# Summing two sets of squares on TensorE as two accumulated terms, in place of an addition on GpSimd

## The reference

```python
q = q / jnp.linalg.norm(q, axis=-1, keepdims=True)        # heads of 64 channels
...
o = jnp.moveaxis(O, 0, 1).reshape(Bx, Lx, NH, HD)
o = o * jax.lax.rsqrt(jnp.mean(o * o, axis=-1, keepdims=True) + EPS) * g
out = o.reshape(Bx, Lx, NH * HD) @ Wo
```

## Time and profile before

| | |
|---|---|
| three runs, median (lowest to highest) | 1305.85 us (1302.28 to 1309.93) |
| the profiled execution | 1308.97 us |
| its span, first to last instruction | 1307.2 us |
| TensorE busy, matmuls | 1155.9 us (88%), 9320 records |
| TensorE busy, weight loads | 979.8 us (75%) |
| VectorE busy | 698.1 us (53%) |
| ScalarE busy | 622.1 us (48%) |
| GpSimd busy | 364.5 us (28%), 294 instructions |
| mean granted TensorE clock | 0.926 |

### The profile page before, as it was taken

The page is one execution under the profiler, slowest core; times in us unless marked ns, Lnnn a source line. Parts: engine busy times, 40 slices in busy tenths (PEclk is TensorE's granted clock), DMA queues, the critical chain, the costliest instruction groups (busy, mean ns, idle before and its releaser), DMA issues.

```text
span 1307.2 us, 25625 instructions
## 1 busy us (share of the span) xinstructions
PE 1155.9 (88%) x9320; PEld 979.8 (75%) x9321; DVE 698.1 (53%) x1195; ACT 622.1 (48%) x1117; POOL 364.5 (28%) x294
## 2 busy tenths in 40 slices
PE   2696889999989899878899899999999999995886
PEld 1465668778777778767788788999999999993665
DVE  2668766765666666666788523333333333333444
ACT  2665546656465646456444634444444444441221
POOL 0315333334252425222012111111111112116542
PEclk9787878999899989989999999999999999997888
DMA  3112020102020102254222411111111111134443
GB/s 123 49 33 65 7 67 17 58 9 73 9 73 10 57 3 95 73 177 141 64 73 84 135 34 34 50 50 49 48 48 48 48 48 48 48 93 134 138 129 102
DMA packets 59529, 86.37 MB, mean 66 GB/s; under 512 B 7233, under 2 KB 49089, under 8 KB 59329
## 3 DMA queue, kind: packets, MB, share of 16 engines
q1 hardware_dynamic: 52160, 65.42, 15.7%
q0 software_dynamic: 7296, 19.93, 5.6%
HBM read 60.16 MB, written 25.17 MB: 65 GB/s over the span
## 4 chain that ended last, share of the span: by engine, by line
PE 68%; DVE 17%; ACT 6%; issue 5%; POOL 2%; DMA 0%; SPq 0%; DVEq 0%; ACTq 0%; POOLq 0%
PE ps L1365 25%; PE ps L1345 23%; DVE W L1523 4%; PE ps L1202 4%; PE ps L1192 3%; PE ps L1356 3%; PE ps L1264 2%; PE ps L1271 2%; PE ps L1423 2%; DVE late_room L1705 1%; DVE W L1615 1%; PE ps L1325 1%; POOL W L804 1%; PE ps L1176 1%; PE ps L1307 1%
## 5 line engine op out<-in xcount | busy, mean ns | idle before, releaser
L1365 PE MATMUL ps<-W,late_room 128*128 (+1 forms) x3264 | 388.5, 278 | 19.6 <-issue 19.0
L1345 PE MATMUL ps<-late_room,W 128*128 128x256 f16 x3072 | 369.6, 280 | 36.2 <-DVE late_room L1705 20.9
L1365 PEld LDWEIGHTS ps<-W,late_room 128*128 128x128 f16 x3264 | 324.9, 100 | 71.3 <-issue 28.3
L1345 PEld LDWEIGHTS ps<-late_room,W 128*128 (+1 forms) x3072 | 305.9, 100 | 87.3 <-DVE late_room L1705 26.0
L1068 ACT ACTIVATE ps<-ps 128x512 f32<-128x512 f32 x272 | 158.7, 583 | 407.4 <-PE ps L1345 358.5
L1705 DVE SCALAR_TENSOR_TENSOR late_room<-ps,late_room 128x512 f16<-128x512 f32 x272 | 181.5, 688 | 249.2 <-ACT late_room L1073 230.7
L1073 ACT ACTIVATE late_room<-ps 128x512 f16<-128x512 f32 x272 | 155.8, 596 | 2.5
L1523 DVE SCALAR_TENSOR_TENSOR W<-W 128x512 f32<-128x512 f32 x144 | 122.1, 849 | 8.7 <-ACT W L941 5.3
L1202 PE MATMUL ps<-W 128*128 128x512 f16 x384 | 101.5, 409 | 1.5 <-DVE W L1699 1.5
L922 ACT COPY W<-ps 128x512 f32<-128x512 f32 x112 | 61.0, 589 | 46.8 <-PE ps L1264 34.6
L904 POOL DMA_INDIRECT W<-ys_d,pos_i x64 | 62.1, 970 | 56.4 <-DVE W L1902 18.3
(11 more groups left out here) (178 smaller groups left out, 1375.4 us busy)
## 6 DMA issues: line engine op xcount, KB each, us to landing
wstage<-in_w_ffn SPq DMA_DIRECT2D x40, 512.0 KB, 3.7
ys_d<-late_room SPq DMA_DIRECT2D x36, 256.0 KB
late_room<-in_x SPq DMA_DIRECT2D x8, 512.0 KB, 4.8
W<-in_x SPq DMA_DIRECT2D x8, 512.0 KB, 4.2
x2n_d<-W SPq DMA_DIRECT2D x8, 512.0 KB, 3.2
base_d<-W SPq DMA_DIRECT2D x8, 512.0 KB, 4.1
late_room<-base_d SPq DMA_DIRECT2D x16, 256.0 KB
acc_d<-late_room SPq DMA_DIRECT2D x12, 256.0 KB
```

What stands on the lines that cost most here:

```text
L1345: last = pe.matmul(up_bank(n, c)[:, f * XT:(f + 1) * XT], weight(slot, d, hw, cols), x_halves[:, hx, d], start=(q == 0), stop=(q == len(pa ...
L1365: last = pe.matmul(down_bank(b)[:, c * D:(c + 1) * D], hs[b][:, hh, f, c * P:(c + 1) * P], weight(slot, DB + f // 4, hw, cols), start=(q = ...
```

## The change

GpSimd's addition goes, with its semaphore `o_sq`. `head_sums` takes any number of terms and accumulates them in PSUM, so that TensorE runs two matmuls, one on `qsqT` and one on `osqT`, where it ran one on their sum. TensorE itself now waits for ScalarE's two semaphores. The call for K ("ssq") still has one term.

```diff
-                if slot == 3:
-
-                    pool.wait_ge(q_sq, DB * (n + 1))
-                    pool.wait_ge(o_own_sq, DB * (n + 1))
-                    pool.tensor_tensor(osqT, osqT, qsqT, ALU.add).then_inc(o_sq, 1)
...
-            def head_sums(dst, src):
+            def head_sums(dst, *terms):
 
                 for k in range(GT):
                     for d in range(DB):
                         at = k * NH + d * (P // HD)
-                        last = pe.matmul(dst[:, at:at + P // HD], src[:, d, k * P:(k + 1) * P], headsel,
-                                         start=True, stop=True)
+                        for q, src in enumerate(terms):
+                            last = pe.matmul(dst[:, at:at + P // HD], src[:, d, k * P:(k + 1) * P], headsel,
+                                             start=(q == 0), stop=(q == len(terms) - 1))
                 return last
...
                 if slot == 5:
 
-                    pe.wait_ge(o_sq, n + 1)
-                    head_sums(fill(tl, n, "oss"), osqT).then_inc(tl.sem_full, 1)
+                    pe.wait_ge(q_sq, DB * (n + 1))
+                    pe.wait_ge(o_own_sq, DB * (n + 1))
+                    head_sums(fill(tl, n, "oss"), qsqT, osqT).then_inc(tl.sem_full, 1)
```

More of the change, by code:

```diff
@@ L502, in build @@
         o_ready = sem("o_ready")
-        o_sq = sem("o_sq")
         o_rms = sem("o_rms")
```

## The result

In twenty runs each the changed kernel takes 1303.4 us (1299.27 to 1305.62) and the kernel before 1306.2 (1302.28 to 1311.62): ratio 0.9971, 95% interval 0.9958 to 0.9984. The forecast was 1311, 5 us more than before; it is 2.8 us less. Two later measurements on two other chips, on which both kernels are 3% faster, gave 0.9949 (0.9931 to 0.9967) and 0.9945 (0.9926 to 0.9964). So the change is a small gain of 0.3 to 0.6%, and the sign of the forecast was wrong.

The account below looks back on a forecast made before the run. TensorE's chain from K's head sums to the turned K, made late by VectorE's block, was taken as the bound. 18.8 - 8.3 - 2.5 - 3.0 = +5.0 us on the median 1305.85 gave 1311 us, range 1301 to 1319.

Parts of the forecast that it names:

- What bounds the kernel: TensorE's work from K's head sums to the turned K is the chain; GpSimd's addition costs mostly by blocking VectorE.
- The added matmuls, 18.8 us: In each group's oss, 8 more matmuls (16 records) on TensorE's chain cost 18.8 us in all.
- The block, 8.3 us: VectorE's convolution step no longer held by the addition in groups 0 to 5, so ScalarE's silu comes earlier: 8.3 us gained.
- The wait in group 7, 2.5 us: TensorE no longer waits for GpSimd's addition before oss in group 7: 2.5 us gained.
- The clock, -3.0 us: TensorE's granted clock: fewer falls after ssq, some new ones after oss, longer low stretches in groups 0 and 1; net -3.0 us.
- two and a half of the four falls gone (-6.9), two new ones (+3.4): Clock falls at ssq in groups 2 to 5 partly vanish, -6.9 us; two new falls after oss cost +3.4 us.
- The half microsecond for longer low stretches: In groups 0 and 1 the low-clock stretches last longer, costing half a microsecond.
- clock holds: Rival: no clock fall left in groups 2 to 5, oss of groups 0 and 1 at full clock; 1299.5 us, chance 0.19.
- with groups 0 and 1 as they are, -3, 1303: Milder case: no fall left in groups 2 to 5, groups 0 and 1 unchanged; -3 us, 1303 us, within the rival's 0.19.
- the prediction's own sign of it: In the trace after the change, none of the old clock falls left would mean this rival has it.
- The rival's reason: TensorE's idle time that precedes each clock fall, ahead of ssq, is cut by two thirds.
- the first rival: Clock falls after the longer oss in each of groups 2 to 6; +11 us, 1317 us, chance 0.27.

Follow-up runs that it names:

- the late addition: Kernel before, with GpSimd's addition also waiting for ScalarE's squares of K, so it starts later: 1283.6 us, ratio 0.9811; again on the third chip 0.9822.
- the two halves: Kernel before, with GpSimd's addition cut into two instructions of 512 elements each: 1264.8 us on the second chip, ratio 0.9975.
- the changed kernel with the wide selector: Changed kernel, with a selector of 128 columns instead of 2 in all head sums: 1296.1 us, ratio 0.9912 to the kernel before.
- The shifted run: Changed kernel, with VectorE's sum over the chunks done twice in group 2 alone: 1267.0 us on the third chip, ratio 0.9997 to the kernel before.
- the one-term trace: Changed kernel with 16 instead of 32 records in oss, Q's squares replaced by a constant EPS: 1283.1 us, ratio 0.9807 to the kernel before.

## Why the prediction was wrong

*What bounds the kernel* was right: TensorE's stretch from ssq to the turned K is the chain (VectorE's 3.20 us wait is unchanged), and the addition costs by VectorE's block, shown by the late addition and by the two halves.

*The added matmuls, 18.8 us*: in the profile all oss together take 33.6 us against 17.9, 15.7 more; the price at full clock (1.79 us a group) was right to 0.1 us. Group 1 was mis-sized: its oss ran at full clock (3.48 us), where I took 3.20 on top of 3.20.

*The block, 8.3 us*: right. ScalarE's idle time before the silu is gone, and TensorE's before ssq fell by 8.8 us in groups 0 to 5 together (to 0.86 us in group 4, about 0.9 forecast).

*The wait in group 7, 2.5 us*: right. From VectorE's sum over the chunks (575.3 before, 570.6 after) to the end of oss (588.06 and 584.27) it is 12.8 us before and 13.7 after, 0.9 more; the sum had 3.59 - 2.51 = 1.1 more.

*The clock, -3.0 us*: this is the step that failed, "two and a half of the four falls gone (-6.9), two new ones (+3.4)". All four went, in three traces of three, and of groups 2 to 6 only group 6 got a new one, in one trace of three. The four were worth a little less than the 11.0 of the prediction: ssq and the feed-forward behind it took 28.1 us in groups 2 to 5 before and 18.4 after, 9.8 less, since an ssq at full clock takes 1.95 us and not 1.68. With -9.8 and +1.7 (L1361 behind oss in group 6 takes 4.31 us for 2.64) the clock term is -8.1, and the sum with every term as measured is 15.7 - 8.8 - 2.5 - 8.1 = -3.7 us. The two profiled executions differ by -5.4, the medians by -2.8. With the clock term alone put right, 8.0 - 8.1 = -0.1, the sum would still not show the gain; the mis-sized group 1 makes the rest. The half microsecond for longer low stretches was wrong as well: around oss the clock is low for 10.2 us in group 0 (6.8 before), but for 3.4 in group 1 (10.2 before).

It was the rival "clock holds" in its milder form ("with groups 0 and 1 as they are, -3, 1303"), which had 0.19 as a whole, and the prediction's own sign of it came: none of the old falls is left. The rival's reason held only in part: the changed kernel with the wide selector gains another 0.4 to 0.6%, so two-column matmuls still cost clock in it, in groups 0 and 1, and in 6 in one trace, but not in 2 to 5 as the first rival had it. That all four went was partly luck of their place in time. The shifted run turned the median by 3.6 us beyond its added work (5.9 - 2.3), about half of the change's 7.0 us on that chip and more than its 2.8 us in the result, so from the lengths of idle time and matmuls this term could not be had to the microsecond.

What stays open: the removal of block and addition is worth 25 us beside the short oss, and lateness, wait and the four falls explain 8.8 + 2.5 + 9.8 = 21.1 at most, for in the one-term trace group 3 still has a fall behind ssq. The other 4 us were not told apart. In that trace the clock is low for 58 us between 115 and 600 us, against 92 before, so fewer falls in groups 0 and 1 and at the groups' ends, which lie differently in every trace, are long enough to hold them.

## What to carry to other kernels

Look for instructions of VectorE that take several times their usual length beside a GpSimd instruction (2.93 us for 0.76 here): no view of waits names them. Moving the GpSimd instruction to where VectorE's next result is not wanted was worth about three times as much (22.8 against 7.0 us on the third chip) as removing it at TensorE's expense. Before work goes from an idle engine to the one on the chain, ask whether the idle engine's instruction can just start later. And the two-column matmuls took little time but left the clock to fall; widening them with columns that nobody reads made both kernels faster.

## What the runs showed of the hardware

- A matmul of 128 columns costs nearly what one of 2 columns costs here, 3.57 us for 32 f32 records against 3.47.
- After the same idle time of 2.60 us, the clock fell behind 16 two-column records and did not behind 16 of 128 columns.
- A GpSimd addition (128 x 1024, f32) holds a VectorE step that starts beside it until it ends, 2.93 us for 0.76. GpSimd's power -1/2 (128 x 16, about 3 us) does not: steps beside it take 0.75 us.
- The kernel before differed by 3% between chips (1309 us on one, 1268 on the two others). From VectorE's last sum over the chunks to the end the changed kernel took 731.2 us at a mean granted clock of 0.95 in the trace of the result and 690.3 us at 0.98 on the second chip, while the attention ahead of it took 570.6 and 567.5 us. Why was not studied.
